# Attention scores in 64-row tiles, mask added on VectorE with the row maximum, denominators sent through DRAM

## The reference

```python
Q, K, V = (proj(Wq, bq), proj(Wk, bk), proj(Wv, bv))          # 16 heads of 16
lam = LAMBDA_MAX * jnp.exp(-ALPHA * u_prev.reshape(Bb))
use_sparse = lam >= SPARSE_THRESHOLD
scores = jnp.einsum('bhqd,bhkd->bhqk', Q, K) * scale
bias = lam[:, None, None, None] * prior_bias[None, None]      # prior_bias is 0 or -1
dense_out = jnp.einsum('bhqk,bhkd->bhqd', jax.nn.softmax(scores + bias, axis=-1), V)
idx = prior_indices[:Ss]                                      # 32 keys of each query
s_scores = jnp.einsum('bhsd,bhskd->bhsk', Q, K[:, :, idx]) * scale
sparse_out = jnp.einsum('bhsk,bhskd->bhsd', jax.nn.softmax(s_scores, axis=-1), V[:, :, idx])
out = jnp.where(use_sparse[:, None, None, None], sparse_out, dense_out)
return out @ Wo.T + bo
```

## Time and profile before

| | |
|---|---|
| Three runs, median (lowest to highest) | 2219.41 us (2218.94 to 2220.04) |
| Profiled execution, span (the page gives no other time of its own) | 2220.5 us |
| Instructions | 42789 |
| PE busy | 2051.3 us, 92% |
| PEld busy | 1652.1 us, 74% |
| DVE busy | 1699.0 us, 77% |
| ACT busy | 1196.2 us, 54% |
| POOL busy | 796.4 us, 36% |
| First row maximum of the second batch | 67.27 us |
| Last residual of the attention layer starts | 936.60 us |

### The profile page before, as it was taken

How to read it: one execution, slowest core, us unless ns; L and a number is a source line. 1 busy time by engine, 2 the same in 40 slices (tenths; PEclk the granted TensorE clock), 3 DMA queues, 4 the chain that set the end, 5 groups by cost and what they waited for, 6 DMA issues and landing times. The chain is left out here.

```text
span 2220.5 us, 42789 instructions
## 1 busy us (share of the span) xinstructions
PE 2051.3 (92%) x14158; PEld 1652.1 (74%) x14158; DVE 1699.0 (77%) x2530; ACT 1196.2 (54%) x2428; POOL 796.4 (36%) x589
## 2 busy tenths in 40 slices
PE   3899999999999999759999999999995999999998
PEld 2566666666666666447777777777774999999997
DVE  6788888888888888577878888887875566666664
ACT  2466565666665666435555555555554555555553
POOL 4645444444455554033333333333340111111111
PEclk8999999999999999879999999999997999999998
DMA  3444444444444444100000000000001222222221
GB/s 92 106 106 107 107 110 110 108 109 108 105 105 106 108 109 104 24 25 1 0 0 0 0 0 0 0 0 0 0 0 59 78 79 70 85 69 80 85 66 60
DMA packets 121171, 137.47 MB, mean 62 GB/s; under 512 B 24240, under 2 KB 89776, under 8 KB 121136
## 3 DMA queue, kind: packets, MB, share of 16 engines
q1 hardware_dynamic: 118576, 128.64, 22.9%
q0 software_dynamic: 2560, 8.39, 1.0%
HBM read 48.35 MB, written 8.39 MB: 26 GB/s over the span
## 5 line engine op out<-in xcount | busy, mean ns | idle before, releaser
L366 DVE TENSOR_REDUCE a_neg_max<-a_s 128x2 f32<-128x512 f32 x512 | 329.1, 683 | 123.4 <-PE a_s L613 121.8
L487 ACT ACTIVATE a_e<-a_t 128x512 f32<-128x512 f32 x512 | 281.2, 610 | 228.4 <-PE a_t L626 228.4
L375 DVE SCALAR_TENSOR_TENSOR a_e<-a_e,a_w_t 128x1024 f32<-128x1024 f32 x256 | 373.6, 1469 | 4.1 <-ACT a_e L487 4.1
L613 PE MATMUL a_s<-a_k_st,a_q_st 96*128 96x256 f32 x1024 | 275.4, 380 | 0.0
L613 PEld LDWEIGHTS a_s<-a_k_st,a_q_st 96*128 96x128 f32 x1024 | 203.5, 199 | 13.7
L610 PE MATMUL a_s<-a_add_m,ident_bf 128*128 128x512 bf16 x512 | 201.8, 394 | 7.9 <-POOL a_add_m L254 5.8
L1695 ACT ACTIVATE c_hid<-c_pH,c_b 128x256 f32<-128x256 f32 x256 | 107.4, 471 | 186.3 <-PE c_pH L1758 185.9
L897 POOL TENSOR_TENSOR b_decayed<-b_table,b_mod_t 128x1024 f32<-128x1024 f32 x64 | 118.6, 1872 | 210.3 <-ACT b_mod_t L1163 203.0
L1317 PE MATMUL b_pS<-b_gated_t,b_decayed 128*128 128x256 f32 x768 | 189.5, 390 | 0.7
L626 PE MATMUL a_t<-a_q_st,a_k_st 97*128 97x512 f32 x512 | 177.1, 426 | 2.6 <-DMA a_q_st<-a_max_row 2.0
L642 PE MATMUL a_v<-a_e,a_v_pad 128*32 128x256 f32 x2048 | 163.6, 392 | 4.5 <-DVE a_e L375 2.1
(11 more groups left out here) (261 smaller groups left out, 5720.4 us busy)
## 6 DMA issues: line engine op xcount, KB each, us to landing
a_q_st<-a_q_hi SPq DMA_DIRECT2D x256, 128.0 KB, 2.4
a_k_st<-a_k_hi SPq DMA_DIRECT2D x256, 64.0 KB, 2.0
a_q_st<-a_q_lo SPq DMA_DIRECT2D x128, 128.0 KB, 2.4
a_xs<-in_xT SPq DMA_DIRECT2D x32, 256.0 KB, 2.8
a_k_st<-a_k_lo SPq DMA_DIRECT2D x128, 64.0 KB, 2.1
x_all<-in_xT SPq DMA_DIRECT2D x32, 256.0 KB, 2.8
c_we<-in_we SPq DMA_DIRECT2D x32, 256.0 KB, 2.7
c_key_t<-in_keyT SPq DMA_DIRECT2D x32, 256.0 KB, 3.2
```

The lines of the kernel that those rows point to most:

```text
L366: dve.tensor_reduce(neg_max[:, qc, head:head + 2], ps_s[b][:], AX.X, ALU.max, negate=True).then_inc(red_done, 1)
L375: dve.scalar_tensor_tensor(out=buf[:], in0=buf[:], scalar=BIG, in1=w_t[par][:, kc].unsqueeze(1).to_broadcast([P, 4, S]), op0=ALU.min, op1= ...
L487: act.activation(e[g % E_BUFS][:, 2 * b:2 * b + 2], ps_t[b][:], ACT.Exp).then_inc(exp_done, 1)
L613: ins = pe.matmul(ps_s[b][:, r], q_st[par][0:96, slot, qc * P:qc * P + P], k_st[par][0:96, slot // 2], start=False, stop=(r == 1))
```

## The change

- **Score tiles.** The stacks of q and k become one tile `st`. Rows 0 to 63 hold one head, rows 64 to 127 another: 16 rows each of high, high and low parts (48 rows), and the maximum in row 48. `score_rows` is four matmuls of 256 columns, two heads at row position 0 and two at 64, and waits for the maxima of all four heads of the group before. `score_cols` likewise: four of 256 columns, after both exponentials of the group before.
- **Mask.** The mask matmul goes. `row_max` is four `tensor_tensor_reduce` of 128x256: PSUM scores plus `add_m` (now float32), written back to PSUM, with the maximum to `top`.
- **Denominators.** `collect`, `spread` and `combine` go. GpSimd issues two DMAs that write the denominators of a batch to DRAM, one that reads them as 128x32, one that writes the reciprocals to DRAM and one that reads them spread over 128 rows. ScalarE issues four DMAs that merge the halves of the heads.
- **Order.** On TensorE `project_q` and `project_k` stand behind `score_cols`. On GpSimd `denominators` stands ahead of `masks` and `spread` ahead of `weights`. On VectorE `normalize` moves from group 4 to 5.
- **Splits.** High parts of q and k are one instruction (ScalarE), low parts one (GpSimd, 128x1024). The stack is still 24 DMAs, each of 16 rows; 8 of the 12 of a half wait for the low parts, before 4 of 12. `maxima` is two DMAs.
- **Setup.** Constants load in the same block as the rest. The counts come from 64 comparisons in bfloat16 (`hot`) and 64 accumulating matmuls.

```diff
+            for done, term, first, step in ((hi_done, 0, 1, 1), (lo_done, 1, 1, 2), (lo_done, 2, 0, 2)):
                 sp.wait_ge(done, n + 1)
+                for r in range(2):
                     for j in (2 * half, 2 * half + 1):
+                        rows = split[64 * r + 16 * j:64 * r + 16 * j + 16, first:first + step + 1:step].bitcast(F32)
+                        sp.dma_start(st[par][64 * r + 16 * term:64 * r + 16 * term + 16, :, j].bitcast(F32), rows)\
+                          .then_inc(d_stack[half], 16)
...
+        def denominators(n):
+            at_least(pool, d_den, n * 16)
+            for half in range(2):
+                pool.wait_ge(raw_done, 2 * n + half + 1)
+                pool.sem_inc(pool_seen, 1)
+                pool.dma_start(den_rows[:, half], raw_v[half][16 * (1 - half)::32].rearrange("j c s -> j (c s)")).then_inc(d_row, 16)
+            pool.wait_ge(d_row, 32 * (n + 1))
+            at_least(pool, rden_done, n)
+            pool.sem_inc(pool_seen, 1)
+            pool.dma_start(den[:], den_rows.rearrange("j h (m k) -> (j h m) k", k=32)).then_inc(d_den, 16)
+
+        def spread(n):
+            pool.wait_ge(rden_done, n + 1)
+            at_least(pool, d_rep, n * 16)
+            pool.sem_inc(pool_seen, 1)
+            pool.dma_start(r_rows.rearrange("j h (m k) -> (j h m) k", k=32), rden[:]).then_inc(d_r, 16)
+            pool.wait_ge(d_r, 16 * (n + 1))
+            at_least(pool, att_done, n)
+            pool.sem_inc(pool_seen, 1)
+            pool.dma_start(r_rep[:].rearrange("p c s -> p (c s)"),
+                           r_rows.rearrange("j h s -> (j h) s").unsqueeze(1).to_broadcast([8, DH, C * S])).then_inc(d_rep, 16)
...
         def body(n, par, proj, maxi, finish):
+            if finish:
+                denominators(n - 1)
             if proj:
                 masks(n + 2, par)
+            if finish:
+                spread(n - 1)
...
-            for b in range(2):
-                dve.wait_ge(s_done, 2 * (n * GROUPS + g) + b + 1)
-                head = 4 * quad + 2 * b
-                dve.tensor_reduce(neg_max[:, qc, head:head + 2], ps_s[b][:], AX.X, ALU.max, negate=True).then_inc(red_done, 1)
+            for r in range(2):
+                for c in range(C):
+                    head = 8 * r + 2 * j + c
+                    dve.tensor_tensor_reduce(out=ps_s[r][:, c], in0=ps_s[r][:, c], in1=add_m[par][:, qc], scale=1.0, scalar=-BIG,
+                                             op0=ALU.add, op1=ALU.max, accum_out=top[:, qc, head:head + 1]).then_inc(red_done, 1)
...
+            if not (isinstance(n, int) and n == 0 and g == 0):
+                pe.wait_ge(red_done, 4 * (n * GROUPS + g))
+            for c in range(C):
+                for r in range(2):
+                    rows = slice(64 * r, 64 * r + 48)
+                    ins = pe.matmul(ps_s[r][:, c], st[par][rows, 0, j, c, qc * P:qc * P + P], st[par][rows, 1, j, c],
+                                    start=True, stop=True, tile_position=(64 * r, 0))
+            ins.then_inc(s_done, 1)
```

456 lines of the change are left out of this document (193 added, 263 removed).

## The result

| | |
|---|---|
| Changed kernel, four runs, median (lowest to highest) | 2434.69 us (2413.36 to 2438.64) |
| Kernel before, four runs on the same chip | 2219.72 us (2218.94 to 2221.75) |
| Ratio, 95% interval | 1.0947 (1.0904 to 1.0989) |
| Profiled execution, span | 2434.1 us (before 2220.5) |

A forecast was written before the change was run, and what follows sets the result against it. TensorE was taken as full, VectorE close with 3.6 us of slack. VectorE's work and waits were to make a batch 29.8 us against 27.0: +87 over 31 batches, setup -5, end +7, so +89, 2308 us; range 2200 to 2375.

The forecast's parts named there:

- the setup: Before the attention loop: an earlier first DMA and new counts were to change the time by -5 us, between -14 and +4.
- the end: After the last batch: four DMA hops instead of two matmul routines and copies, +7 us, between +4 and +10.
- VectorE's side: Attention loop: with pairs at 0.435 us and weighings at 1.41, VectorE's work rises 3.0 us a batch, to 26.1.
- The waits afterwards: VectorE's waits at the seam (passage between batches): 1.4 us at the first group, 2.0 at the second, 3.4 a batch.
- Rival 3: Attention loop: TensorE's granted clock falls, doubling its steps at the seam; +2.5 us a batch, 2390 us; chance 0.07.
- Rival 2: Attention loop: GpSimd's chain with its DRAM trips becomes the bound; 31.3 us a batch, +133, 2355 us; chance 0.20.
- The middle groups: Groups away from the seam: a weighing covers the next scores, so VectorE has no wait over 0.2 us.
- TensorE's side: Attention loop: TensorE's work falls from 26 to 19.1 us a batch, between 15.5 and 24.6; no term of the sum.
- GpSimd's work on weighings: GpSimd's wide instructions slowing VectorE's weighings: counted as nothing; up to 6 us a batch if all coincided, 2.1 back if none.

The follow-up runs named there:

- e5: Changed kernel with only its normalisation undone (collect, spread and combine back, no DMAs for the denominators): 2263.53 us.
- e3: Changed kernel without GpSimd's five DMAs of the denominators and their waits, so normalisation is left out: 2286.33 us.
- e11: Changed kernel without GpSimd's five denominator DMAs (normalisation left out) and with project_q and project_k ahead of score_cols: 2258.95 us.
- e6: Changed kernel with its normalisation undone as in e5, and project_q and project_k ahead of score_cols: 2268.13 us.
- e1: Changed kernel with 16 added matmuls of zeros a batch where TensorE waits: 2392.76 us.
- e8: Kernel before the change, with only project_q and project_k moved behind score_cols: 2256.03 us.
- e4: Kernel before the change, with only the mask moved to VectorE in add-and-maximum pairs, no mask matmul: 2235.66 us.
- e7: As e6, with the mask back as a matmul on TensorE and one 128x512 reduction a bank on VectorE: 2261.84 us.

## Why the prediction was wrong

- **The sum, term by term.** The loop was to cost +87, the setup -5, the end +7, and what follows nothing. Measured: the loop +200.8 (194.2 and the 6.6 of its first two batches), the setup -0.5, inside -14 to +4, the end +7.0, and the layers behind +6.4 with the same code. (In the runs these layers take 1283 to 1294 us; why is open.) So the miss lies in the loop.
- **VectorE's side: right in kind, the terms off both ways.** Pairs start 0.383 us apart (505.19 to 505.58 and so on), not 0.435: 12.3 us a batch for 13.9. The weighing's mean is 1.61 us instead of 1.49, a step of 1.53 for 1.41: 12.3 for 11.3. The sum of its work is 25.4 measured for 26.4 with the gaps. VectorE over 90% busy was named as the sign of the forecast; it was 74%.
- **"The waits afterwards": the step that failed.** 3.4 us a batch was forecast and 8.6 came, because the seam was priced with TensorE at full clock. At the second group the chain was the right one, from the maxima's DMA over columns and `project_q` to the next scores: 4.67 for 2.0. From the first maxima on, the columns began 0.45 us later than said, and `project_q` took 3.48 for 1.54. Of these 1.94, 0.38 is a misreading: the 1.54 was read where the next matmuls overlapped in the records, while at full clock it takes 1.92 in the changed kernel (`project_k`, 511.13 to 513.05), and for the eight matmuls of `project_out` the forecast itself had 1.8. The other 1.56 are the clock. At the first group the path was misjudged too: 3.38 came for the 1.4 of "weighing, values, scores", and what VectorE waited for was `project_out` at half clock and the values behind it, which the forecast did not count.
- **Rival 3, the clock: the mechanism that came, argued away by comparing busy shares.** 0.54 at 44% busy and 64% in the new loop seemed safe, and it got 0.07. Its sign, a granted clock under 0.9, was there: 0.75. Its price, +2.5 us a batch, was too low if anything: the two projections of the seam alone take 1.56 and 1.79 us more than at full clock, and by e5 TensorE's records are 6.4 us a batch longer than they need be, not all of it on the seam.
- **Rival 2, the trips: the right part of the change, by a path that was not taken.** It said that the low parts and with them the stacks and the maxima's DMAs come too late, with 1 to 2 us of slack. The reciprocal came at 517.08 for 514 and the low parts ended at 527.95, but the stacks still landed 3.8 us early, and none of the signs that it named came: no idle time of either engine ended by a stack DMA, `a_den` or `a_r_rep`, and the low parts ended 10.6 us before the next batch's scores, not under 8. Yet e3 and e5 show that without the trips 148 to 171 us of the 215 go. That the rival looked at the trips is to its credit; that they cost about what it said (+133) is luck.
- **The frame was a fault of its own.** The rivals had chances as if one or another would come. The edits do not add: the order is worth 3.8 us a batch with the trips, 0.7 without (e3 to e11) and -0.2 in e5 to e6. Both edits shorten TensorE's waits and its records together. The reading that fits is a loop: waits ahead of the seam lower the clock, and the lower clock lengthens `project_out` and `project_q`, on which VectorE and so TensorE wait. Only a part of it is shown by an experiment that touches nothing else (e1).
- **"The middle groups" wait for nothing: nearly.** VectorE waits 0.58 us in one of them (524.15), where none over 0.2 was said. TensorE's waits for the maxima there (0.83, 0.71 and 1.51 us) were named as a sign of the forecast.
- **TensorE's side.** A group of four took 0.34 us at full clock for the 0.46 taken, inside 0.23 to 0.8, no term of the sum, as said.
- **GpSimd's work on weighings, "counted as nothing".** It cost 1.0 us a batch, of up to 6.

Two things are open. One is how the trips lead to the waits: in the profiles the low parts fall on a weighing ahead of `project_out` with them and earlier in the batch without, but no run moved that meeting and nothing else. The other is how the last 40 us of e5 split. e8 gives 1.15 us a batch to the order and e4 0.30 to the pairs in the kernel before, and e6 and e7 show that the order gives nothing in 64-row tiles, whose joint release stands in its place.

## What to carry to other kernels

When a change opens slack on the fullest engine, work out every chain around the loop with the durations of the slower clock as well; here both projections at the seam doubled. If two rivals lengthen the same chain, price them together. Check a suspected chain in the list of waits before building on it: a path with 4 us to spare costs nothing, however late it looks. Before moving a transfer in its queue, ask which transfer it will then share the DMA engines with. And where one instruction replaces another engine's, the best share is often neither none nor all: here two or three of eight groups.
